# Turning the state update of a gated linear attention kernel: values stationary, keys moving

## The chip, the cores and the metric

The kernel runs on one core of one Trainium2 chip. The time is that of the device for one execution, in microseconds; where several runs were made, their median. Matrix products run on TensorE (PE), elementwise work on VectorE (DVE) and ScalarE (ACT), gathers and scatters are issued by GpSimd (POOL), and SyncE (SP) issues the other DMAs.

## The reference

A layer norm without weights gives `xn` for 4 sequences of 2048 tokens of width 256. The result is `x + attention(xn) + experts(xn)`. The attention is gated and linear, with 8 heads, keys of 128 and values of 64:

```python
state = at[..., None, None] * state + kt[..., None] * vt[:, :, None, :]   # per head: 128 x 64
out_t = jnp.einsum('bhk,bhkv->bhv', qt, state)
...
return out * jax.nn.sigmoid(x @ Wog) @ Wo
```

The experts are 64, of which each token takes 8 by a grouped top-k; each expert takes at most 256 tokens, in the order of their positions, through `silu(g) * u` and a down product, weighted and summed.

## The kernel before, in words

The sequences are cut in 16 chunks of 128 tokens; a step works on one chunk of all four sequences (b = 0 to 3). In a step, the scan over time becomes matrix products: the scores of a chunk are weighted by decays (`Dt`) and multiplied by the values, the state from earlier chunks is read through scaled queries (`outputs`, L773 to L791), and the state is brought forward (`update`, L794): for each head and sequence the transposed keys, weighted by the decay to the chunk's end (`kw`), times the values. `kw` comes from `keys_back` (L755), which transposes the keys on PE into bank 3, and `keys_weighted`, which is on ACT (L980) in the steps of kind norm, count and slots and on DVE (L1379) in the expert steps. `update` writes bank 6, two heads side by side, and DVE's `pair_state` (L1412) decays the state of a pair of heads and adds the bank.

Beside the attention each step carries other work; its kind says which. Steps 0 to 4 ("norm") normalise and route three chunks each. Step 5 ("count") counts the experts' tokens, step 6 ("slots") builds the lists of slots: POOL compares (`reach_group`), PE multiplies pairs of experts (`slot_pair`, L693) and DVE counts them (`count_pair`, L1337). Steps 7 to 14 ("experts") run eight experts each, one a slot; step 15 is "last".

Within a step (`step` of PE, L889) there are eight slots, s = 1 to 8, one for a head. A slot transposes keys and makes scores for head s - 1, transposes the tokens of an expert (L842), projects the next head's queries and keys (L719), runs the expert's gate and up product (L852), in even slots the outputs of a pair, and then the update of head s - 1. Slot 8 has no query and key projection. Every engine runs its own instructions in the written order; semaphores join them (`kw_cp`: weighted keys are there; `u_ps`: the update's products; `state_up`; `oi_ps`: outputs; `v_cp`; `wo_cp`). Places 0 to 4 in `beside` are the points between which the other work of a slot is put.

In an expert slot ACT copies the projections and the transposed tokens, then takes the sigmoid of the expert's gate (`expert_gate`, L1072), then rounds the next expert's weights (`weights_high_e`, L1063). DVE makes the hidden values (L1454, L1456), the weights' remainder (`weights_low_e`, L1460), the gated outputs (L1410), the state (L1423, L1426), and the tokens' remainder (`tokens_low_e`, L1465), for which the next expert product waits. SP issues loads in one order (L416): `load_carry` after the outputs of a pair, `load_decay`, and `next_expert` (L411) after an expert's down product.

Of the kernel before, what the change touches and what calls it, by code (L numbers as in the profile page):

```python
# [13 lines left out]
ALU = mybir.AluOpType  # L14
# [55 lines left out]
def at(c, per, k):  # L70

    return c * per + k


def build(nc, x_in, Wq, Wk, Wv, Wo, Wg, bg, Wog, gate_w, gate_bias, w_gate, w_up, w_down, out):
    with ExitStack() as ctx:
# [42 lines left out]
        kw = sb("kw", [P, B, DK])  # L119
# [158 lines left out]
        state_scaled, state_up = sem("state_scaled"), sem("state_up")  # L278
        gate_done, g_high, g_low = sem("gate_done"), sem("g_high"), sem("g_low")
# [28 lines left out]
        def tokens_bank(c, k):  # L308
            return bank[6] if is_first(c) and k == 1 else bank[7]

# [321 lines left out]
        def _(pe):  # L632
# [122 lines left out]
            def keys_back(c, h):  # L755
                pe.wait_ge(qk_cp, at(c, 16, 2 * h + 2))
                if not (isinstance(c, int) and c == 0 and h == 0):
                    pe.wait_ge(kw_cp, at(c, 8, h))
                for b in range(B):
                    last = tr(bank[3][:, b * P:(b + 1) * P], kT[:, h % 2, b * P:(b + 1) * P], ident[:, :])  # L760
                last.then_inc(kt_ps, 1)
# [32 lines left out]
            def update(c, h):  # L794
                pe.wait_ge(kw_cp, at(c, 8, h + 1))
                if h > 0 and h % 2 == 0:
                    pe.wait_ge(state_up, at(c, 4, h // 2))
                if h == 0 and not (isinstance(c, int) and c == 0):
                    pe.wait_ge(wo_cp, 4 * c)
                for b in range(B):  # L800
                    lo = (h % 2) * B * DV + b * DV
                    last = mm(bank[6][:, lo:lo + DV], kw[:, b, :], V[:, b, h * DV:(h + 1) * DV],  # L802
                              start=True, stop=True)
                if h % 2:
                    last.then_inc(u_ps, 1)

            def out_proj(c, b):

                to = out_bank(c, b)
                if b == 0:  # L810
                    pe.wait_ge(g_low, 4 * c)
                if isinstance(c, int) and c == C - 1:
                    pe.wait_ge((kw_cp, state_up)[b // 2], (8, 4)[b // 2] * (C - 1))
                elif b == 1:
                    pe.wait_ge(state_up, 4 * c)
                elif b > 1:
                    pe.wait_ge(wo_cp, 4 * (c - 1) + b - 1)
                for j in range(KO):
                    for i, (part, other) in enumerate(PARTS):
                        last = mm(to, gT[:, part, j, b * P:(b + 1) * P], wo[:, other, j, :],  # L820
                                  start=(j + i == 0), stop=(j == KO - 1 and i == 2))
                last.then_inc(wo_ps, 1)
# [66 lines left out]
            def step(c, kind):  # L889
# [19 lines left out]
                if not is_last(c):  # L909
                    keys_back(c, 0)  # L910
# [6 lines left out]
                for s in range(1, H + 1):  # L917
                    if s > 1 and not is_last(c):
                        keys_back(c, s - 1)
# [9 lines left out]
                    if s in og_slots(kind):  # L929
                        proj_og(c, kind, og_slots(kind).index(s))  # L930
# [5 lines left out]
                    if s < H:  # L936
                        proj_qk(c, kind, s, 1)
                    beside(c, kind, s, 2)
                    if s % 2 == 0:
                        outputs(c, s // 2 - 1)  # L940
                    beside(c, kind, s, 4)
                    if not is_last(c):
                        update(c, s - 1)
# [21 lines left out]
        def _(act):  # L965
# [14 lines left out]
            def keys_weighted(c, h):  # L980
                act.wait_ge(scan_done, at(c, 8, h + 1))
                act.wait_ge(kt_ps, at(c, 8, h + 1))
                for b in range(B):
                    ins = f(kw[:, b, :], bank[3][:, b * P:(b + 1) * P], ACT.Copy, scale=Dt[:, h, b, P - 1:P])
                ins.then_inc(kw_cp, 1)
# [65 lines left out]

            def outs_high(c, p):
                act.wait_ge(gate_done, at(c, 4, p) + 1)
                f(gT[:, 0, p, :], gated[:, :], ACT.Copy).then_inc(g_high, 1)
# [19 lines left out]
            def beside(c, kind, s, place):  # L1074
# [21 lines left out]
                if kind == "experts" and s > 0 and place == 2:  # L1096
                    expert_gate(c, s - 1)
                    if s < H:
                        weights_high_e(c, s)

            def step(c, kind):
# [24 lines left out]
                for s in range(1, H + 1):  # L1126
# [10 lines left out]
                    if s < H:  # L1137
                        qk_copy(c, kind, s, 1)
                    if kind == "norm" and s % 3 == 0:
                        normalise(STEP_N * c + 1 + s // 3)  # L1140
                    if s in og_slots(kind) and kind == "count":
                        og_gate(c, kind, og_slots(kind).index(s))
                    beside(c, kind, s, 2)
                    if s % 2 == 0:
                        outs_high(c, s // 2 - 1)
# [13 lines left out]
        def _(dve):  # L1159
# [219 lines left out]
            def keys_weighted(c, h):  # L1379
                dve.wait_ge(scan_done, at(c, 8, h + 1))  # L1380
                dve.wait_ge(kt_ps, at(c, 8, h + 1))
                tt(kw[:, :, :], bank[3][:, :].rearrange("p (b d) -> p b d", b=B),
# [29 lines left out]
            def pair_state(c, p):  # L1412

                both = state[:, 2 * p:2 * p + 2].rearrange("p u b v -> p (u b) v")
                added = bank[6][:, :].rearrange("p (r v) -> p r v", v=DV)
# [10 lines left out]
                tt(both, both, added, ALU.add).then_inc(state_up, 1)  # L1426
# [103 lines left out]
            def step(c, kind):  # L1530
# [8 lines left out]
                for s in range(1, H + 1):  # L1539
# [30 lines left out]
                    if s % 2 == 0:  # L1570
                        pair_gated(c, s // 2 - 1)
                        if not is_last(c):
                            pair_state(c, s // 2 - 1)
# [52 lines left out]
```

## Time and profile before

| | us |
|---|---|
| median of 3 runs | 1312.73 (1310.9 to 1312.99) |
| profiled execution | 1313.61 |
| its span | 1311.9 |
| PE busy | 1285.5 |
| DVE busy | 954.0 |
| ACT busy | 556.4 |
| POOL busy | 505.6 |

The page gives each engine's busy time, the chain of work that ended last and the costliest groups; the timeline gives start and length of instructions, merged where they are of one kind. PE's records overlap: a record's length is its latency, and what it costs in a stream is read from start to start. A bracket at the end of a timeline row is the idle time of the engine before it and what ended it. PEld rows are the weight loads.

### The profile page before, as it was taken

To read this page: it belongs to the slowest core of one execution; us is meant where nothing else is said; L and a number is where in the kernel's file an instruction comes from. 1 tells how busy PE (TensorE), PEld (TensorE's weight loads), DVE (VectorE), ACT (ScalarE), POOL (GpSimd) and SP (SyncE) were. 2 spreads that over 40 slices of the span, in tenths; PEclk is the share of its full clock that TensorE was granted. 3 is DMA by queue.
4 is the path that set the end of the run, shared out by engine and by line. 5 is a ranking of instruction groups with operands and counts; after the bars stand their busy time and mean duration, and the time that the engine had idled before them with its cause. 6 is when DMAs were issued, how large, how long until landed. Compare 5 with 4: busy or idle time off the path is not lost.

```text
span 1311.9 us, 27512 instructions
## 1 busy us (share of the span) xinstructions
PE 1285.5 (98%) x9478; PEld 1131.3 (86%) x9478; DVE 954.0 (73%) x2431; ACT 556.4 (42%) x1139; POOL 505.6 (39%) x405
## 2 busy tenths in 40 slices
PE   7999999999999999999999999999999999999999
PEld 6788888888888887799898898998988989989987
DVE  6987978888896659957667577676785776767844
ACT  6566556555653433333333333333333333333322
POOL 2110100110010039637356366274573653745710
PEclk8999999999999999999999999999999999999999
DMA  7565535363442212157576486575774756656755
GB/s 239 178 241 189 176 113 174 101 193 118 153 166 70 81 49 81 34 166 165 126 168 172 99 196 138 129 170 128 171 171 107 194 130 159 165 125 160 173 175 194
DMA packets 124919, 194.66 MB, mean 148 GB/s; under 512 B 12016, under 2 KB 98608, under 8 KB 124592
## 3 DMA queue, kind: packets, MB, share of 16 engines
q1 hardware_dynamic: 94384, 147.99, 34.7%
q0 software_dynamic: 30464, 45.83, 19.1%
q8 instruction: 32, 0.52, 0.2%
q14 instruction: 39, 0.32, 0.1%
HBM read 148.62 MB, written 57.74 MB: 157 GB/s over the span
## 4 chain that ended last, share of the span: by engine, by line
PE 80%; DVE 12%; issue 3%; DMA 2%; POOL 1%; ACT 1%; SPq 0%; DVEq 0%; ACTq 0%; POOLq 0%
PE bank L719 21%; PE bank L802 7%; PE bank L769 7%; PE bank L852 7%; PE bank L734 6%; PE bank L820 6%; PE bank L751 5%; PE bank L787 5%; PE bank L861 4%; PE bank L790 4%; PE bank L760 3%; PE bank L842 2%; DVE Dt L1367 2%; DVE At L1388 2%; POOL sel_all L599 1%
## 5 line engine op out<-in xcount | busy, mean ns | idle before, releaser
L575 POOL DMA_INDIRECT acc<-arena,idx_all x128 | 216.5, 1692 | 129.2 <-issue 68.0
L567 POOL DMA_INDIRECT arena<-table,idx_all x132 | 161.0, 1220 | 201.6 <-ACT share L1060 146.6
L719 PE MATMUL bank<-xp,wq 128*128 128x512 f32 x768 | 215.0, 415 | 0.0
L719 PE MATMUL bank<-xp,wk 128*128 128x512 f32 x768 | 203.9, 400 | 0.2 <-DVE wk L1288 0.2
L719 PEld LDWEIGHTS bank<-xp,wk 128*128 128x128 f32 x768 | 141.1, 188 | 34.1 <-DVE wk L1288 0.6
L719 PEld LDWEIGHTS bank<-xp,wq 128*128 128x128 f32 x768 | 141.0, 190 | 28.6 <-issue 0.5
L1367 DVE TENSOR_TENSOR_SCAN Dt<-decay,eye_b 128x512 f32<-128x512 f32 x128 | 158.1, 1236 | 0.6 <-DMA decay<-decay_dram 0.6
L769 PE MATMUL bank<-qT,kT 128*128 128x128 f32 x1024 | 136.2, 276 | 2.5 <-DVE At L1388 2.5
L1040 ACT ACTIVATE qT<-bank 128x512 f32<-128x512 f32 x128 | 76.6, 598 | 133.8 <-PE bank L719 133.8
L769 PEld LDWEIGHTS bank<-qT,kT 128*128 128x128 f32 x1024 | 125.8, 193 | 3.4 <-DVE At L1388 2.8
L802 PEld LDWEIGHTS bank<-V,kw 128*128 128x128 f32 x960 | 117.5, 191 | 11.7 <-issue 9.8
L802 PE MATMUL bank<-V,kw 128*128 128x64 f32 x960 | 126.8, 275 | 0.0
L1040 ACT ACTIVATE kT<-bank 128x512 f32<-128x512 f32 x128 | 76.5, 597 | 114.8 <-PE bank L719 114.5
L1388 DVE TENSOR_TENSOR At<-bank,Dt 128x512 f32<-128x512 f32 x128 | 87.7, 685 | 34.7 <-PE bank L769 32.9
L544 POOL DMA_DIRECT2D table<-arena x16 | 12.4, 776 | 250.1 <-DVE arena L1272 250.1
L787 PE MATMUL bank<-At,V 128*64 128x128 f32 x1024 | 101.2, 279 | 7.6 <-DVE At L1388 7.6
L1454 DVE TENSOR_TENSOR arena<-bank,arena 128x256 f32<-128x256 f32 x64 | 27.2, 425 | 108.3 <-ACT arena L1072 108.3
L852 PEld LDWEIGHTS bank<-xgT,wgu_p 128*128 128x128 f32 x768 | 97.8, 188 | 9.0 <-issue 3.6
L734 PE MATMUL bank<-wv,xp 128*128 128x512 f32 x384 | 104.6, 408 | 0.2 <-DVE xp L1282 0.2
L751 PE MATMUL bank<-xp,wog 128*128 128x512 f32 x384 | 101.7, 400 | 0.0
L852 PE MATMUL bank<-xgT,wgu_p 128*128 128x256 f32 x768 | 99.5, 279 | 2.0 <-DVE xgT L1465 1.9
L820 PEld LDWEIGHTS bank<-wo,gT 128*128 128x128 f32 x720 | 93.2, 188 | 5.5
(160 smaller groups left out, 2262.1 us busy)
## 6 DMA issues: line engine op xcount, KB each, us to landing
decay<-decay_dram SPq DMA_DIRECT2D x64, 512.0 KB, 5.6
carry<-decay_dram SPq DMA_DIRECT2D x60, 512.0 KB, 4.6
arena<-in_L_attn_x_dram SPq DMA_DIRECT2D x16, 512.0 KB, 4.4
table<-arena SPq DMA_DIRECT2D x16, 512.0 KB, 3.7
xT_dram<-arena SPq DMA_DIRECT2D x16, 512.0 KB, 3.0
arena<-in_L_ffn_w_gate_dram SPq DMA_DIRECT2D x64, 128.0 KB
arena<-in_L_ffn_w_up_dram SPq DMA_DIRECT2D x64, 128.0 KB
arena<-in_L_ffn_w_down_dram SPq DMA_DIRECT2D x64, 128.0 KB
```

The lines of the kernel that those rows point to most:

```text
L567: pool.indirect_dma_start(out=xg[:, e % 2, j, :], out_offset=None, in_=table[:, :], in_offset=bass.IndirectOffsetOnAxis(ap=idx_all[:, e, j ...
L575: pool.indirect_dma_start(out=acc[:, :], out_offset=bass.IndirectOffsetOnAxis(ap=idx_all[:, e, j:j + 1], axis=0), in_=yb[:, e % 2, j, :], ...
L719: last = mm(to[:, :], w[:, part, k, h * DK:(h + 1) * DK], xp[:, other, k, :], start=(k + i == 0), stop=(k == KD - 1 and i == 2))
L734: last = mm(to[:, :], xp[:, part, k, b * P:(b + 1) * P], wv[:, other, k, :], start=(k + i == 0), stop=(k == KD - 1 and i == 2))
L751: last = mm(to[:, :], wog[:, part, k, j * P:(j + 1) * P], xp[:, other, k, :], start=(k + i == 0), stop=(k == KD - 1 and i == 2))
L769: last = mm(bank[2][:, b * P:(b + 1) * P], kT[:, h % 2, b * P:(b + 1) * P], qT[:, h % 2, b * P:(b + 1) * P], start=True, stop=True)
L787: last = mm(bank[5][u * DV:(u + 1) * DV, b * P:(b + 1) * P], V[:, b, h * DV:(h + 1) * DV], At[:, u, b, :], start=True, stop=is_first(c))
L802: last = mm(bank[6][:, lo:lo + DV], kw[:, b, :], V[:, b, h * DV:(h + 1) * DV], start=True, stop=True)
L820: last = mm(to, gT[:, part, j, b * P:(b + 1) * P], wo[:, other, j, :], start=(j + i == 0), stop=(j == KO - 1 and i == 2))
L852: last = mm(expert_bank[j % 2][:, m * CAP:(m + 1) * CAP], wgu_p[:, part, m, k * I:(k + 1) * I], xgT[:, other, k * CAP:(k + 1) * CAP], star ...
L1040: f(dst[:, h % 2, :], bank_of(kind, "qk"[which], h)[:, :], ACT.Copy, scale=scale).then_inc(qk_cp, 1)
L1367: dve.tensor_tensor_scan(Dt[:, h, :, :].rearrange("p b t -> p (b t)"), decay[:, (h // 2) % 2, (h % 2) * BP:(h % 2 + 1) * BP], eye_b[:, :, ...
```

## The change

From the count step to the last expert step (kinds count, slots, experts) the update of a pair of heads is formed the other way round. The values are the stationary operand, 64 columns on one half of the array for each head of the pair; the weighted keys move, 128 columns; the products of both heads and four sequences fill bank 3 (`update_turned`), ahead of the outputs of the pair. ACT copies the bank to SBUF (`update_copy`), into the second of now two buffers of `kw`. After the outputs PE transposes the copy back, four blocks of 128 x 128, into bank 6 (`update_back`), and DVE adds it in the order in which the blocks lie. `keys_back` waits for the copy before it writes bank 3 again. In the expert steps `weights_high_e` comes after `update_copy` on ACT; in count PE's gate projection comes after the second projection of the slot. The first product of the last step waits for `ut_cp`.

```diff
-        kw = sb("kw", [P, B, DK])
+        kw = sb("kw", [P, 2, B, DK])
+        added_t = kw[:, 1, :, :]
...
+        def turned(kind):
+            return kind in ("count", "slots", "experts")
...
-            def keys_back(c, h):
+            def keys_back(c, kind, h):
                 pe.wait_ge(qk_cp, at(c, 16, 2 * h + 2))
                 if not (isinstance(c, int) and c == 0 and h == 0):
                     pe.wait_ge(kw_cp, at(c, 8, h))
+                if turned(kind) and h % 2 == 0:
+                    wait_past(pe, ut_cp, 4 * (c - S_COUNT) + h // 2)
...
+            def update_turned(c, p):
+
+                pe.wait_ge(kw_cp, at(c, 8, 2 * p + 2))
+                pe.wait_ge(v_cp, 4 * c + 4)
+                for b in range(B):
+                    for u in range(2):
+                        h = 2 * p + u
+                        last = mm(bank[3][u * DV:(u + 1) * DV, b * P:(b + 1) * P], V[:, b, h * DV:(h + 1) * DV],
+                                  kw[:, u, b, :], start=True, stop=True)
+                last.then_inc(ut_ps, 1)
+
+            def update_back(c, p):
+
+                pe.wait_ge(ut_cp, 4 * (c - S_COUNT) + p + 1)
+                if p > 0:
+                    pe.wait_ge(state_up, at(c, 4, p))
+                else:
+                    pe.wait_ge(wo_cp, 4 * c)
+                for b in range(B):
+                    last = tr(bank[6][:, b * P:(b + 1) * P], added_t[:, b, :], ident[:, :])
+                last.then_inc(u_ps, 1)
...
-                    pe.wait_ge((kw_cp, state_up)[b // 2], (8, 4)[b // 2] * (C - 1))
+                    pe.wait_ge((ut_cp, state_up)[b // 2], 4 * (C - 1 - (0, S_COUNT)[b < 2]))
...
-                    if s in og_slots(kind):
+                    if s in og_slots(kind) and kind != "count":
                         proj_og(c, kind, og_slots(kind).index(s))
...
                     if s < H:
                         proj_qk(c, kind, s, 1)
+                    if s in og_slots(kind) and kind == "count":
+                        proj_og(c, kind, og_slots(kind).index(s))
                     beside(c, kind, s, 2)
+                    if s % 2 == 0 and turned(kind):
+                        update_turned(c, s // 2 - 1)
                     if s % 2 == 0:
                         outputs(c, s // 2 - 1)
                     beside(c, kind, s, 4)
-                    if not is_last(c):
+                    if s % 2 == 0 and turned(kind):
+                        update_back(c, s // 2 - 1)
+                    if kind == "norm":
                         update(c, s - 1)
...
+            def update_copy(c, p):
+                act.wait_ge(ut_ps, 4 * (c - S_COUNT) + p + 1)
+                f(added_t.rearrange("p b d -> p (b d)"), bank[3][:, :], ACT.Copy).then_inc(ut_cp, 1)
...
                 if kind == "experts" and s > 0 and place == 2:
                     expert_gate(c, s - 1)
-                    if s < H:
-                        weights_high_e(c, s)
+                if kind == "experts" and 0 < s < H and place == 3:
+                    weights_high_e(c, s)
...
+                    if s % 2 == 0 and kind in ("count", "slots"):
+                        update_copy(c, s // 2 - 1)
...
                     beside(c, kind, s, 2)
+                    if s % 2 == 0 and kind == "experts":
+                        update_copy(c, s // 2 - 1)
+                    beside(c, kind, s, 3)
                     if s % 2 == 0:
                         outs_high(c, s // 2 - 1)
...
+                summed, added = both, bank[6][:, :].rearrange("p (r v) -> p r v", v=DV)
+                if turned(kind):
+                    summed = state[:, 2 * p:2 * p + 2]
+                    added = bank[6][:, :].rearrange("p (b u v) -> p u b v", b=B, u=2)
...
-                tt(both, both, added, ALU.add).then_inc(state_up, 1)
+                tt(summed, summed, added, ALU.add).then_inc(state_up, 1)
```

## Rows read from the trace of the kernel before

**Rows 1.** The page: busy time by engine, and the chain that ended last.
```profile
PE 1285.5 (98%) x9478; PEld 1131.3 (86%) x9478; DVE 954.0 (73%) x2431; ACT 556.4 (42%) x1139; POOL 505.6 (39%) x405
...
PE 80%; DVE 12%; issue 3%; DMA 2%; POOL 1%; ACT 1%; SPq 0%; DVEq 0%; ACTq 0%; POOLq 0%
```

**Rows 2.** Windows: length, busy PE, PEld, DVE, ACT, POOL, clock, DMA share, GB/s.
```profile
468.00:552.00 84.00, 80.28 (x598) 63.50 (x596) 68.37 (x335) 26.30 (x60) 64.76 (x64) 0.98 0.15 55
552.00:1247.00 695.00, 693.00 (x5124) 623.59 (x5122) 480.71 (x813) 246.75 (x488) 384.38 (x265) 1.00 0.63 152
```

**Rows 3.** Groups: line, engine, out<-in, shapes, count, busy us, mean ns, idle.
```profile
L1040 ACT ACTIVATE qT<-bank 128x512 f32<-128x512 f32 x128 | 76.6, 598 | 133.8 <-PE bank L719 133.8
...
L802 PEld LDWEIGHTS bank<-V,kw 128*128 128x128 f32 x960 | 117.5, 191 | 11.7 <-issue 9.8
...
L787 PEld LDWEIGHTS bank<-At,V 128*64 128x64 f32 x1024 | 61.4, 136 | 19.8 <-issue 6.0 <-DVE carry L1400 5.2 <-DVE At L1388 3.9
```

**Rows 4.** Timeline of an odd expert slot: start, length, engine, line, operation.
```profile
836.20 1.00 PE L802 MATMUL bank<-V,kw 128*128 128x64 f32 x8
837.03 0.61 PE L760 MATMUL bank<-ident,kT 128*128 128x128 f32 x4
837.48 1.06 PE L769 MATMUL bank<-qT,kT 128*128 128x128 f32 x8
```

**Rows 5.** Timeline of an even expert slot, PE with ACT and DVE.
```profile
862.77 0.44 PE L787 MATMUL bank<-At,V 128*64 128x128 f32 x4
...
863.15 0.62 ACT L1067 ACTIVATE wgu_p<-arena 128x512 fp32r<-128x512 f32 x1
...
863.47 0.39 PE L790 MATMUL bank<-carry,state 128*64 128x128 f32 x4
...
864.35 0.39 PE L790 MATMUL bank<-carry,state 128*64 128x128 f32 x4
864.66 1.10 PE L802 MATMUL bank<-V,kw 128*128 128x64 f32 x8
864.78 0.69 DVE L1410 TENSOR_TENSOR gated<-bank,og 128x512 f32<-128x512 f32 x1
...
865.61 0.61 PE L760 MATMUL bank<-ident,kT 128*128 128x128 f32 x4
```

**Rows 6.** Timeline: slots 7 and 8 of an expert step without late weights.
```profile
628.17 1.54 PE L852 MATMUL bank<-xgT,wgu_p 128*128 128x256 f32 x12
...
632.98 0.69 DVE L1465 TENSOR_TENSOR xgT<-bank,xgT 128x512 fp32r<-128x512 f32 x1
...
634.40 1.53 PE L852 MATMUL bank<-xgT,wgu_p 128*128 128x256 f32 x12
```

**Rows 7.** Waits from 559 to 1247 us: in total, times, longest.
```profile
ACT wgu_p L1067 <- DMA arena<-in_L_ffn_w_down_dram: 16.8, 22, 2.2
...
PE bank L852 <- DVE xgT L1465: 1.9, 3, 1.0
```

**Rows 8.** Timeline: slot 8 of an expert step with late weights.
```profile
808.69 0.68 DVE L1465 TENSOR_TENSOR xgT<-bank,xgT 128x512 fp32r<-128x512 f32 x1
...
809.52 1.61 PE L852 MATMUL bank<-xgT,wgu_p 128*128 128x256 f32 x12 [0.69 <-DVE xgT L1465]
```

**Rows 9.** Timeline of SP's queue: slots 6 and 7 of the same step.
```profile
796.31 0.35 SPq L390 DMA_DIRECT2D carry<-decay_dram  x1
...
799.98 0.38 SPq L395 DMA_DIRECT2D arena<-in_L_ffn_w_gate_dram  x1
```

**Rows 10.** The slots step: a window of DVE, and rows of the timeline.
```profile
510.00:530.00 20.00, 19.86 (x105) 1.00 0.14 54
...
535.21 0.69 DVE L1410 TENSOR_TENSOR gated<-bank,og 128x512 f32<-128x512 f32 x1 [0.57 <-PE bank L790]
...
545.16 1.11 PE L760 MATMUL bank<-ident,kT 128*128 128x128 f32 x4
...
546.07 1.91 PE L769 MATMUL bank<-qT,kT 128*128 128x128 f32 x8
```

More of the change, by code:

```diff
@@ L278, in build @@
         state_scaled, state_up = sem("state_scaled"), sem("state_up")
+        ut_ps, ut_cp = sem("ut_ps"), sem("ut_cp")
         gate_done, g_high, g_low = sem("gate_done"), sem("g_high"), sem("g_low")
@@ L801, in update @@
                     lo = (h % 2) * B * DV + b * DV
-                    last = mm(bank[6][:, lo:lo + DV], kw[:, b, :], V[:, b, h * DV:(h + 1) * DV],
+                    last = mm(bank[6][:, lo:lo + DV], kw[:, h % 2, b, :], V[:, b, h * DV:(h + 1) * DV],
                               start=True, stop=True)
@@ L909, in step @@
                 if not is_last(c):
-                    keys_back(c, 0)
+                    keys_back(c, kind, 0)
                 scores(c, 0)
@@ L918, in step @@
                     if s > 1 and not is_last(c):
-                        keys_back(c, s - 1)
+                        keys_back(c, kind, s - 1)
                     if s > 1 and not is_last(c):
@@ L983, in keys_weighted @@
                 for b in range(B):
-                    ins = f(kw[:, b, :], bank[3][:, b * P:(b + 1) * P], ACT.Copy, scale=Dt[:, h, b, P - 1:P])
+                    ins = f(kw[:, h % 2, b, :], bank[3][:, b * P:(b + 1) * P], ACT.Copy, scale=Dt[:, h, b, P - 1:P])
                 ins.then_inc(kw_cp, 1)
@@ L1381, in keys_weighted @@
                 dve.wait_ge(kt_ps, at(c, 8, h + 1))
-                tt(kw[:, :, :], bank[3][:, :].rearrange("p (b d) -> p b d", b=B),
+                tt(kw[:, h % 2, :, :], bank[3][:, :].rearrange("p (b d) -> p b d", b=B),
                    Dt[:, h, :, P - 1:P].broadcast_to([P, B, DK]), ALU.mult).then_inc(kw_cp, 1)
@@ L1410, in pair_gated, with pair_state @@
                 tt(gated[:, :], bank[5][:, :], og[:, p, :], ALU.mult).then_inc(gate_done, 1)
-            def pair_state(c, p):
+            def pair_state(c, kind, p):
                 both = state[:, 2 * p:2 * p + 2].rearrange("p u b v -> p (u b) v")
-                added = bank[6][:, :].rearrange("p (r v) -> p r v", v=DV)
+                summed, added = both, bank[6][:, :].rearrange("p (r v) -> p r v", v=DV)
+                if turned(kind):
+                    summed = state[:, 2 * p:2 * p + 2]
+                    added = bank[6][:, :].rearrange("p (b u v) -> p u b v", b=B, u=2)
                 if is_first(c):
@@ L1572, in step @@
                         if not is_last(c):
-                            pair_state(c, s // 2 - 1)
+                            pair_state(c, kind, s // 2 - 1)
                     beside(c, kind, s, 4)
```

## The prediction

> **What bounds the kernel now.** I read the page's share of busy time and its chain of waits first: the tensor engine (PE) is busy 98% of the span and carries 80% of the chain that ended last, the vector engine (DVE) 12% [rows 1]. An average over stages could hide a stretch in which PE is not the limit, so the windows come next. From 552 to 1247 us, the eight steps that also run the experts, PE is busy for 693.0 of 695 us while DVE has 481 and ScalarE (ACT) 247: an engine microsecond saved on PE is a microsecond of time there, unless a wait comes up behind it. From 468 to 552 us, mostly the step that builds the slot lists, PE has 80.3 of 84 us, but DVE counts without a break, 19.86 of 20 us in its middle [rows 2, 10]: PE's work is hidden there. Then the timeline of PE, for what one head's update costs and what follows it, and last the waits of two places, since that is where a faster PE would collide.
>
> **What is removed.** In a turned step the four products of a head are issued with the keys stationary, 128 columns, and 64 columns of values moving. The trace has two matmul records for each (fp32), 8 a head. Their weight loads take 191 ns in a record, those of half the columns 136 to 137 [rows 3]. By starts, the odd slot's update occupies PE from 836.20 to 837.03, 0.83 us, the even slot's from 864.66 to 865.61, 0.95 us [rows 4, 5]. A pair costs 1.78 us.
>
> **What is added on PE.** The turned product has V as stationary operand on 64 columns, alternating between the halves, and 128 moving columns: that is exactly the first half of the outputs (L787). There a group of four records (two halves, two records each) starts 0.22 us after the one before: from 863.47 to 864.35 lie four such steps, 0.88 us [rows 5]. A turned pair has 16 records, so four groups, 0.88 us. The change from whole to half array and back (0.31 us from the start of the last half group to the update, where 0.22 would be its own) is paid once at each end of the outputs today, and once at each end of turned product plus outputs afterwards, so it adds nothing. The four transposes back are the kind of L760: 0.45 us from 837.03 to 837.48 [rows 4]. Together 1.33 us, a saving of **0.45 us a pair**. The steps from count to the last expert step are ten, so 40 pairs and 18.0 us at most: 14.4 in the expert steps, 1.8 in count, 1.8 in slots.
>
> The row says that a transpose costs PE 0.11 us in a stream, although each record lasts longer because they overlap. A rule of the Trainium skill speaks against this (TensorE: Matmul & The Clock Gate, Part 4, PE-mode transpose): about 275 ns for a transpose in a kernel's context, and the fast clock does not engage for it. By that, four would take 1.10 us, a pair would lose 0.20 and 40 pairs 8 us, for 1321. The starts of rows 4 contradict it for this stream, with whole expert windows at a granted clock of 1.00, and I go by them.
>
> **The copy and the order.** On ACT one copy of a bank to SBUF is added per pair, of the shape that takes 598 ns [rows 3]. In an even expert slot PE would begin the turned product at 862.77 and end it 0.88 later, at 863.65; a consumer starts some 0.2 us after its producer (gated at 864.78, while the last group that it needs starts at 864.35 and lasts 0.22), so the copy runs from 863.86 to 864.46. PE meanwhile does the outputs, and reaches the transposes at 863.65 + (864.66 - 862.77) = 865.54 [rows 5]. Cover 0.9 us: the new wait costs nothing; if the copy were that much later, PE would stand still and everything behind it too. The expert's sigmoid stands before it on ACT, waits only for the expert product that ends at 862.77, and is over when the weights' copy starts at 863.15. Behind it is now the rounding copy of the next weights (863.15 before, 864.46 after, 1.3 later), and DVE's subtraction behind that, so gated and the state follow 1.2 us later. PE's own even slot is 0.38 us longer (0.88 + 0.45 - 0.95), so DVE falls back by 0.8 against PE, into idle time (481 of 695 busy); nothing is charged, and up to 0.8 us a pair is its price without that cover. The add on DVE reads the same 512 elements in another order; I take no change, between nothing and a tenth more of one instruction off the path. The second buffer of keys, the swapped gate projection in the one count step and the exchanged semaphore at the last step change no amount of work: nothing.
>
> **What eats the gain in the experts.** The slot saved 0.83 us is the odd one, the loss of 0.38 lies in the even one. After slot 7 comes slot 8, which has no query and key projection, and DVE's chain to the split tokens is nearly its bound. In a good step the two expert products start at 628.17 and 634.40, 6.23 us apart; the split tokens that the second needs are ready at 632.98 + 0.69 = 633.67, and a start follows a release by 0.15 (808.69 + 0.68 to 809.52) [rows 6, 8]. So DVE allows 5.65 and PE would want 6.23 - 0.83 = 5.40: 0.25 lost. In four of the eight steps the weights come late by DMA, and the product starts just as it is released (three of them with an idle time, 1.9 us in all [rows 7], as at 809.52 [rows 8]); there the whole 0.83 is lost. 4 x 0.25 + 4 x 0.83 = 4.3 us. Then the queue of SP: it issues the carry and decay loads when the outputs of slot 6 end (796.31), the weights after slot 7's expert down product (799.98) [rows 9]. The first moves 0.88 later and the second only 0.38, so half a megabyte twice stands 0.5 us closer ahead of the weights. ACT waited for weights 22 times already [rows 7]. Bounds for this: 0, and 8 x 0.5 = 4.0; I take 2.5, since it is the place where waits are already frequent. Expert steps: 14.4 - 4.3 - 2.5 = **7.6 us**.
>
> **Count and slots.** In count PE is the limit and no slack is short: **1.8 us**. In slots DVE is the limit, so what PE saves is not seen, and the turned product now stands 0.88 us ahead of outputs for which DVE already waits (0.57 us at 535.21). Ends: a gain of 1.8, and a loss of 4 x 0.88 = 3.5 plus one more stretch at the slow clock; there is one now, after a wait, in which four transposes need 0.91 us from 545.16 (to 546.07) and their row 1.11 instead of 0.61 [rows 10]; the window's mean clock of 0.98 over 84 us says that it cost 0.02 x 84 = 1.7 us. From -1.8 to +5.2; I take a **loss of 1.3 us**, nearer to the middle, because only the even slots whose start is tied to DVE or GpSimd pass it on.
>
> **Sum.** 7.6 + 1.8 - 1.3 = 8.1 us. The profiled execution took 1313.61 us (span 1311.9); less 8.1 is 1305.5. The median of the runs is 0.88 lower (1312.73), so 1304.6 us.
>
> **The rivals.**
> A, the transposes run slowly: with the 0.91 us of rows 10 a pair costs 0.88 + 0.91 = 1.79, nothing is gained anywhere, and slots lose 1.3: 1314. For it: they are the most of what is new on PE. Against: all transposes of the expert steps [rows 4, 5]. 0.03.
> B, the gain is eaten by waits: slot 8 takes 1.33 in all eight steps (10.6), the other places as in the worst slots case (5.2): 18.0 - 1.8 - 10.6 - 5.2 = 0.4 us gained, 1312.3. For it: rows 7 to 9. Against: DVE idles for 31% of the expert steps. 0.07.
> C, slower: weights arrive late not by 0.5 but by 2 us more in each expert step, because the loads ahead of them and the indirect transfers share the same queues' bandwidth. PE then waits at slot 8 for 0.83 + 2.0 in each of eight steps, 22.6 us, against 14.4 + 1.8 - 1.3 of the rest: 7.7 slower, 1320.4. It decides from 14.9 / 8 = 1.86 us a step. For it: 16.8 us of waits for these weights already. Against: the loads' own time is short against a slot of 10 us, and the fall back on the queue is only 0.5. 0.05.
> D, slower: the alternating halves do not overlap when the keys move. At the 0.104 us a record of the full array (0.83 / 8) a pair costs 1.66 + 0.45 = 2.11, 0.33 more than now, 13 us over 40 pairs: 1326. Against: L787 has the same operands' shapes at 0.055 a record. 0.04.
>
> **From cases to numbers.** The forecast has 0.81. Its own range: best 18.0 - 1.0 (every step a good one, slots gaining), about 1296; worst 1312. 8 in 10 needs less: I give 1298.5 to 1310. What a measurement can tell from no change is about 0.2%, 2.6 us. Faster than 1310.1: nearly all of the forecast, 0.82; same, from A, B and the forecast's worst end, 0.09; slower, C and D, 0.09.
>
> **What would show it.** In the changed trace the turned matmuls (128*64, 128 moving) should have groups of four 0.22 apart; the transposes of the added tile start to start 0.11; no idle time of PE before them, and the copy over before the outputs are. The first matmul of the expert product in slot 8 should have an idle time in all eight steps, 0.3 to 1.5 us, released by the split tokens. The slots stretch should be as long as now or longer, with PE waiting more. I am wrong if PE waits for the copy, if the turned groups run at 0.4, or if PE's idle time in the expert steps stays under 3 us (then the time is nearer to 1299) or passes 15.

## The result: slower by 0.44%, where a gain was forecast

| | before | after |
|---|---|---|
| median, us (runs) | 1313.03 (11) | 1319.47 (11) |
| lowest to highest | 1310.90 to 1315.15 | 1315.33 to 1323.51 |
| profiled execution (span) | 1313.61 (1311.9) | 1316.75 (1315.1) |

The ratio is 1.0044, 95% interval 1.0031 to 1.0057. The forecast was 1304.6 with a range to 1310.0: wrong, in its sign too. The profiled execution of after is 2.7 us under its median, so its trace shows 3.2 us of the 6.4. All times are those of runs at the high granted clock; one run of slots_after (1402.9 us) and one of the kernel before beside it (2110.22 us, mean granted clock 0.556) are left out.

The page after, as in [rows 1]: busy time by engine, and the chain that ended last, by engine.

```profile
PE 1269.2 (97%) x9638; PEld 1109.3 (84%) x9638; DVE 953.4 (73%) x2431; ACT 579.2 (44%) x1179; POOL 503.7 (38%) x405
...
PE 74%; DVE 12%; DMA 5%; issue 4%; POOL 2%; ACT 1%; SPq 1%; DVEq 0%; ACTq 0%
```

PE is busy for 16 us less and gives up six points of the chain; DMA goes from 2 to 5%, and the next line of the page of the profile names it: the expert weights, `arena<-in_L_ffn_w_down_dram`. The windows of after, columns as in [rows 2]:

```profile
468.00:552.00 84.00, 75.36 (x570) 58.62 (x570) 67.09 (x333) 26.43 (x61) 64.24 (x64) 0.98 0.16 52
552.00:1247.00 695.00, 683.34 (x5243) 608.21 (x5244) 479.29 (x811) 265.46 (x521) 379.20 (x263) 1.00 0.63 151
```

In the expert steps PE now stands still for 11.7 of 695 us, where it was 2.0. The waits of after from 559 to 1250 us, as in [rows 7] (total, times, longest):

```profile
ACT wgu_p L1106 <- DMA arena<-in_L_ffn_w_down_dram: 29.0, 21, 2.6
...
PE bank L881 <- DVE xgT L1512: 9.8, 11, 1.7
```

ACT waited 16.8 us for the weights before and waits 29.0 now; PE waited 1.9 us for the split tokens and waits 9.8, of which six times and 7.9 us in slot 8.

The even slot of after, PE and ACT, against [rows 4, 5]. L821 is `update_turned`, L833 `update_back`, L1089 `update_copy`, L797 the second half of the outputs, L767 `keys_back`, L881 the gate and up product, L1106 `weights_high_e`:

```profile
620.25 1.09 PE L821 MATMUL bank<-kw,V 128*64 128x128 f32 x16
621.17 0.39 PE L794 MATMUL bank<-At,V 128*64 128x128 f32 x4
...
622.70 0.39 PE L797 MATMUL bank<-carry,state 128*64 128x128 f32 x4
623.02 0.66 PE L833 MATMUL bank<-ident,kw 128*128 128x128 f32 x4
623.51 0.60 PE L767 MATMUL bank<-ident,kT 128*128 128x128 f32 x4
...
621.39 0.60 ACT L1089 ACTIVATE kw<-bank 128x512 f32<-128x512 f32 x1 [0.65 <-PE bank L821]
```

The turned product takes 0.92 us (forecast 0.88), the four transposes 0.49 (0.45), and the copy is over at 621.99, 1.0 us before PE comes to the transposes (0.9). What was costed on PE and ACT came within 0.04 us a piece.

Where the time of an expert step went is seen by adding PE's groups of instructions from start to start, so that a wait counts to the group ahead of it. Means of seven expert steps, from slot 1 of the first to slot 1 of the last, us a step:

| group | before | after |
|---|---|---|
| update; turned product + transposes back | 7.08 | 3.70 + 1.89 |
| outputs and `keys_back` | 11.13 | 10.91 |
| slot 8: gate projection up to the expert product | 1.95 | 2.68 |
| slot 8: token transposes up to the down product | 0.44 | 0.74 |
| query and key projections, with waits behind them | 23.57 | 23.94 |
| expert products and down products, with waits behind them | 16.95 | 17.16 |
| whole step | 86.94 | 86.88 |

The first two rows save 1.71 us a step, 13.7 in eight; the other four lose 1.61; the groups not listed differ by 0.04. By another mark, the split of a step's tokens on DVE (x_split) to the next one, the eight expert steps last 694.2 us before and 695.0 after (the last of them, outside the means above, 86.5 and 88.1), the count step 76.3 and 74.9, the slots step 87.2 and 89.3. With 1.2 us by which the untouched norm steps and 0.5 by which the last step came out longer in this one trace, that is the 3.2 us: 0.8 - 1.4 + 2.1 + 1.2 + 0.5. (The slots step's 87.2 is high for the old update: before_again, sp_before and carry_late have 86.5, so the change costs 2.8 us there.)

### The profile page after: what moved, and what is told of

The parts are those of the page before. It is cut to its first block, busy times and chain, and to the rows that moved or that the text cites. A ratio compares the mean times of both kernels' runs of the same rounds, so it can differ in the third digit from the quotient of the medians.

```text
span 1315.1 us, 27947 instructions
## 1 busy us (share of the span) xinstructions
PE 1269.2 (97%) x9638; PEld 1109.3 (84%) x9638; DVE 953.4 (73%) x2431; ACT 579.2 (44%) x1179; POOL 503.7 (38%) x405
## 4 chain that ended last, share of the span: by engine, by line
PE 74%; DVE 12%; DMA 5%; issue 4%; POOL 2%; ACT 1%; SPq 1%; DVEq 0%; ACTq 0%
PE bank L724 19%; PE bank L849 6%; PE bank L739 6%; PE bank L776 6%; PE bank L881 6%; DMA arena<-in_L_ffn_w_down_dram 5%; PE bank L756 5%; PE bank L794 4%; PE bank L797 4%; PE bank L890 4%; PE bank L821 3%; PE bank L767 3%; PE bank L871 2%; DVE At L1432 2%; POOL sel_all L604 2%
## 5 line engine op out<-in xcount | busy, mean ns | idle before, releaser
L580 POOL DMA_INDIRECT acc<-arena,idx_all x128 | 220.5, 1723 | 148.8 <-issue 57.8
L572 POOL DMA_INDIRECT arena<-table,idx_all x132 | 155.6, 1179 | 186.1 <-ACT share L1099 128.8
L881 PEld LDWEIGHTS bank<-xgT,wgu_p 128*128 128x128 f32 x768 | 97.0, 188 | 20.6 <-issue 16.3
L881 PE MATMUL bank<-xgT,wgu_p 128*128 128x256 f32 x768 | 100.7, 280 | 9.8 <-DVE xgT L1512 9.8
L549 POOL DMA_DIRECT2D table<-arena x16 | 12.4, 777 | 249.4 <-DVE arena L1316 249.4
L849 PE MATMUL bank<-wo,gT 128*128 128x256 f32 x720 | 94.6, 280 | 0.0
L797 PE MATMUL bank<-carry,state 128*64 128x128 f32 x960 | 93.9, 273 | 0.0
L604 POOL TENSOR_SCALAR sel_all<-arena 64x256 bf16<-64x256 bf16 x64 | 64.2, 1018 | 65.4 <-DVEq L1379 55.3
```

The source lines that it names most:

```text
L572: pool.indirect_dma_start(out=xg[:, e % 2, j, :], out_offset=None, in_=table[:, :], in_offset=bass.IndirectOffsetOnAxis(ap=idx_all[:, e, j ...
L580: pool.indirect_dma_start(out=acc[:, :], out_offset=bass.IndirectOffsetOnAxis(ap=idx_all[:, e, j:j + 1], axis=0), in_=yb[:, e % 2, j, :], ...
L797: last = mm(bank[5][u * DV:(u + 1) * DV, b * P:(b + 1) * P], state[:, 2 * p + u, b, :], carry[:, p % 2, u, b, :], start=False, stop=True)
L881: last = mm(expert_bank[j % 2][:, m * CAP:(m + 1) * CAP], wgu_p[:, part, m, k * I:(k + 1) * I], xgT[:, other, k * CAP:(k + 1) * CAP], star ...
```

## Why the weights are late: one step with a wait, one without

SyncE's queue in after, slots 6 and 7 of two expert steps, with the rounding that needs the weights. Columns: start, length, engine, line, operation. L395 is the carry load, L389 the decay load, L400 the first load of an expert's weights:

```profile
624.58 0.35 SPq L395 DMA_DIRECT2D carry<-decay_dram  x1
625.18 0.33 SPq L389 DMA_DIRECT2D decay<-decay_dram  x1
626.48 0.38 SPq L400 DMA_DIRECT2D arena<-in_L_ffn_w_gate_dram  x1
...
633.74 0.63 ACT L1106 ACTIVATE wgu_p<-arena 128x512 fp32r<-128x512 f32 x1 [2.56 <-DMA arena<-in_L_ffn_w_down_dram]
...
636.21 0.68 DVE L1512 TENSOR_TENSOR xgT<-bank,xgT 128x512 fp32r<-128x512 f32 x1
...
637.04 1.61 PE L881 MATMUL bank<-xgT,wgu_p 128*128 128x256 f32 x12 [1.67 <-DVE xgT L1512]
...
796.60 0.34 SPq L395 DMA_DIRECT2D carry<-decay_dram  x1
797.20 0.33 SPq L389 DMA_DIRECT2D decay<-decay_dram  x1
799.82 0.38 SPq L400 DMA_DIRECT2D arena<-in_L_ffn_w_gate_dram  x1
...
805.39 0.63 ACT L1106 ACTIVATE wgu_p<-arena 128x512 fp32r<-128x512 f32 x1 [1.15 <-DMA arena<-in_L_ffn_w_down_dram]
```

In the second step the weights are issued 3.22 us behind the carry load (before: 3.67 [rows 9]) and rounded 5.6 us after issue. In the first they stand 1.90 behind it and are rounded 7.3 after issue; from there DVE's remainder, its split of the tokens and the product follow, and PE stands for 1.67 us. The eight steps of after fall in two classes for the load of slot 7: distances (from the issue of the carry load to that of the weights) of 3.0 to 3.4 with 5.0 to 5.7 us to the rounding, and 1.5 to 2.0 with 7.0 to 7.6, four of each. Before, all eight distances are 3.7, with 4.4 to 6.6.

The forecast had the step from 3.67 to 3.2, and there the first class lies. It did not have the second: there the carry load is issued 1.88 us after the start of the last output products (622.70 to 624.58), in the other step 0.57 (796.03 to 796.60), as before (795.74 to 796.31). The carry load waits for nothing but these products. Such late signals are found without the change too (last section); the change took 0.5 us of the distance that had to cover them.

## The experiments

Three theories stood at the start. **Q**, the queue: outputs that end 0.9 us later let SyncE issue carry and decay, a megabyte, right ahead of an odd slot's weights. **V**: the rounding of the weights, moved behind the copy on ACT, pushes DVE back. **S**: the change itself makes the semaphores of PE's products arrive late. The ratios are to the kernel before as it ran beside them (medians 1313.33 for the first four, 1314.30 for the next four, 1314.70 for the last two). Each trace is one execution, up to 6 us off its kernel's median (sp_after 1313.27), so where a trace and a median disagree by a few microseconds the median decides.

| run | median, us | ratio | 95% interval |
|---|---|---|---|
| sp_after | 1306.98 | 0.9953 | 0.9936 to 0.9970 |
| sp_before | 1312.45 | 0.9997 | 0.9986 to 1.0008 |
| weights_first | 1314.75 | 1.0016 | 1.0001 to 1.0032 |
| turned_early | 1317.84 | 1.0033 | 1.0018 to 1.0047 |
| carry_late | 1320.94 | 1.0055 | 1.0038 to 1.0072 |
| sp_wfirst | 1308.58 | 0.9963 | 0.9949 to 0.9976 |
| sp_noslots | 1306.49 | 0.9943 | 0.9924 to 0.9962 |
| before_again | 1312.02 | one run | |
| early_noslots | 1318.93 | 1.0032 | 1.0021 to 1.0044 |
| slots_after | 1307.47 | 0.9959 | 0.9944 to 0.9974 |

### The loads in another order, in both kernels

In the expert steps SyncE issues the weights of slots 3, 5 and 7 one place earlier, ahead of carry and decay. The same edit in after (sp_after) and in before (sp_before), here its second half:

```diff
...
                 if kind == "experts":
-                    next_expert(c, 3)
                     next_expert(c, 4)
+                    next_expert(c, 5)
                 load_carry(c + 1, 0)
...
-                    for j in range(5, ends):
+                    for j in range(6, ends):
```

> The changed kernel with one edit: in the expert steps SyncE issues the weights for slots 3, 5 and 7 before, not after, the carry and decay loads of half a megabyte each. In the changed kernel ACT waits 29.0 us for weights (21 times), before it 16.8, and the products of slot 8 start just as the split tokens release them. Theory Q (the queue: the outputs, and with them the carry load, come later and stand right ahead of the weights): ACT's waits for weights fall under 5 us, the idle time of PE before the expert products falls from 9.8 to under 4, the expert steps shorten by 8 to 12 us, so about 1308. Rival V (the vector engine's chain, put back by the later rounding of the weights, is what starves slot 8): the waits for DMA go, the time does not, 1315 to 1320. Rival S (semaphores of PE arrive late in slots 4 and 6, 1 to 2.3 us after the matmul): gated still starts up to 2.7 us after the last output group; the time moves by less than 4 us.

> The kernel before with the same edit of SyncE's order as sp_after: weights for slots 3, 5 and 7 ahead of the carry and decay loads. It has 16.8 us of ACT waits for weights, but only 1.9 us of them reach PE before the expert products. All theories: 1 to 2 us faster than before at most, or the same. If it is as much faster as sp_after is than the changed kernel, the queue's order is no part of what the change cost.

Measured: after gains 12.5 us by it (1319.47 to 1306.98) and is now faster than before; before gains 0.9, inside its interval. The waits of sp_after, in which the rounding is at L1108 and the product at L883:

```profile
ACT wgu_p L1108 <- DMA arena<-in_L_ffn_w_down_dram: 5.9, 5, 2.5
...
PE bank L883 <- DVE xgT L1514: 3.5, 4, 1.7
```

29.0 us of waits for weights became 5.9, 9.8 of PE's became 3.5, and the expert steps 689.7 us long, 5.3 less where Q expected 8 to 12; this trace is 6.3 us over its median. Q holds: the same edit is worth 12.5 us with the turned update and nothing measurable without it, and with it the turned update is a gain.

### The delay alone, put into the kernel before

carry_late keeps the old update and lets SyncE's carry load of an expert step wait for the update's products instead of the outputs':

```diff
-                sp.wait_ge(oi_ps, 4 * c + p - 1)
+                sp.wait_ge(u_ps if late else oi_ps, 4 * c + p - 1)
```

> The kernel before with one wait exchanged in the expert steps: SyncE's carry load waits for the update that follows a pair's outputs, not for the outputs, so the carry and decay loads are issued 1.3 us later and stand that much closer ahead of the weights; no engine does other work. Theory Q: ACT's waits for weights rise from 16.8 to 25 to 32 us, slot 7 to slot 8 of the expert products goes from 6.57 us on average to 7.2 or more, and the time rises by 4 to 9 us, to about 1319. If the late outputs cost nothing by way of the queue (rivals V and S), the time stays within 2 us of 1313.

Measured: 1320.94, 6.6 us slower. Its queue and its waits:

```profile
798.28 0.34 SPq L390 DMA_DIRECT2D carry<-decay_dram  x1
798.88 0.33 SPq L384 DMA_DIRECT2D decay<-decay_dram  x1
800.92 0.38 SPq L395 DMA_DIRECT2D arena<-in_L_ffn_w_gate_dram  x1
```

```profile
ACT wgu_p L1067 <- DMA arena<-in_L_ffn_w_down_dram: 41.3, 29, 3.9
...
PE bank L852 <- DVE xgT L1465: 8.0, 9, 2.8
```

The distance is 2.6 us instead of 3.7 (1.0 less, not the 1.3 expected; 2.6 in most steps, down to 1.9 in slot 7 and 1.1 in slot 5), and that alone makes the picture of after: ACT's waits 41.3, more than the 25 to 32 expected, PE's 8.0. The expert steps last 702.6. No instruction of PE, ACT or DVE was touched, and no wait for the carry or decay loads themselves appears on them, so the place of these loads ahead of the weights is enough as a cause.

### The rounding ahead of the copy again

```diff
                     expert_gate(c, s - 1)
-                if kind == "experts" and 0 < s < H and place == 3:
-                    weights_high_e(c, s)
+                    if s < H:
+                        weights_high_e(c, s)
```

> The changed kernel with one part undone: ACT rounds the next expert's weights right after the expert's sigmoid again, ahead of the copy of the turned update. Theory Q: the weights that are late are those of odd slots, in which there is no copy, so nothing is gained: within 2 us of the changed kernel. Rival V: the vector engine gets the even slots' weights 1.3 us earlier, its fall back of 0.8 us a pair is gone, and the expert steps shorten by 4 to 8 us. If the copy becomes late instead, PE waits before the transposes and it gets slower.

> The changed kernel with both edits: weights for the odd slots ahead of the carry and decay loads on SyncE, and ACT rounding the weights ahead of the copy of the turned update. The first alone gave 1307.0, the second alone 1314.8, the changed kernel 1319.5. If the queue (Q) and the vector engine's chain (V) are two separate causes, their gains add, and with slot 8 bound by the chain at 5.65 us in place of 6.4 it comes to 1302 to 1305. If V acted only through late weights it stays at 1307.

On after it brings 4.7 us (1314.75), on sp_after nothing (1308.58 against 1306.98, the wrong way). The 4.7 us lie in V's range (4 to 8); Q had expected at most 2 and missed. So the place of the rounding matters while the weights are late, and by the times not otherwise: V is a part of the price of late weights, as sp_wfirst's expectation had it for this outcome. In the profile of weights_first the waits for weights stay at 30.5 us and PE's at 9.3.

### The turned product ahead of the expert product

```diff
+                    if s % 2 == 0 and kind == "experts":
+                        update_turned(c, s // 2 - 1)
                     beside(c, kind, s, 2)
-                    if s % 2 == 0 and turned(kind):
+                    if s % 2 == 0 and turned(kind) and kind != "experts":
                         update_turned(c, s // 2 - 1)
```

> The changed kernel with the turned product of the expert steps moved from just behind the expert product to just ahead of it (after the second projection), its copy on ACT right after the projection's. The same work, but the dense stream of half-array matmuls is cut in two, and the outputs follow the expert product directly as they did before. Theory Q: the outputs end no earlier against the weights of the next slot, so ACT's waits for weights stay at 25 to 30 us, but slot 8's product is called 0.9 us later and so idles less: 3 to 6 us faster. Theory S with density as its cause: the last output group to gated falls back to 0.44 us in slots 4 and 6, the carry load follows at 0.57, and the waits for weights fall to some 17: 8 to 12 us faster, about 1308. If neither matters it stays at 1319.

> sp_noslots (weights ahead of the carry loads, slots step as before) with the turned product of the expert steps moved ahead of the expert product, and its copy right behind the projection's. Theory: with the weights on time, slot 8 is bound by VectorE's chain to the split tokens (5.65 us from slot 7's product by the trace of before; 6.04 measured in sp_noslots), and now PE fills 0.9 us of that wait with the turned product. The expert steps (685.2 us in sp_noslots) shorten by up to 8 x 0.4 to 8 x 0.9, so 1300 to 1304. Rival: the outputs' end and the copy's order matter more, no gain: 1306. Against it speaks that the same move alone gave only 1317.8 from 1319.5.

Both missed. turned_early takes PE's waits for tokens from 9.8 to 0.6 us, keeps ACT's for weights at 25.5, and is at 1317.84, 1.6 us faster than after where Q expected 3 to 6; early_noslots, the same on top of the best version, is 12.4 us slower than it. PE's starts in early_noslots (L826 turned product, L886 expert product, L799 outputs), and below them in sp_noslots, in the old order:

```profile
615.21 1.09 PE L826 MATMUL bank<-kw,V 128*64 128x128 f32 x16
616.23 1.65 PE L886 MATMUL bank<-xgT,wgu_p 128*128 128x256 f32 x12
617.81 0.44 PE L799 MATMUL bank<-At,V 128*64 128x128 f32 x4
```

```profile
806.26 1.65 PE L886 MATMUL bank<-xgT,wgu_p 128*128 128x256 f32 x12
807.84 1.09 PE L826 MATMUL bank<-kw,V 128*64 128x128 f32 x16
808.77 0.39 PE L799 MATMUL bank<-At,V 128*64 128x128 f32 x4
```

Ahead of the outputs, which use half the columns as it does itself, the turned product costs 0.93 us; ahead of the full-width expert product 1.02. Each pair now has two more changes between half and whole array; by the starts the projection ahead of them costs 0.09 us more, the turned product 0.10, the expert product 0.08, the outputs 0.05: 0.32 us a pair, 10 us in 32 pairs. The prediction had counted these changes and found that the order chosen adds none; this pair shows what they would have cost. The Trainium skill (TensorEngine Tiling (Array Packing), Key Properties) says that a change of tiling mode drains the array; these rows fit, at 0.05 to 0.1 us for a group beside such a change, but do not show the drain itself. The expert steps of early_noslots are 20.0 us longer than those of sp_noslots (705.2 and 685.2). The other 10 us are longer gaps behind the projections of slot 7 (0.35 a step), behind the token transposes of slot 8 (0.2) and at the step's end (0.55 a step, the transposes back up to the value projection); why these came was not followed further, and the one trace is 3.5 us over its median.

### The slots step as before, and the turned product elsewhere in it

sp_noslots is sp_after with the slots step's updates as they were; slots_after is sp_after with the turned product behind the outputs in that step:

```diff
-            return kind in ("count", "slots", "experts")
+            return kind in ("count", "experts")
```
```diff
-                    if s % 2 == 0 and turned(kind):
+                    if s % 2 == 0 and turned(kind) and kind != "slots":
                         update_turned(c, s // 2 - 1)
                     if s % 2 == 0:
                         outputs(c, s // 2 - 1)
+                    if s % 2 == 0 and kind == "slots":
+                        update_turned(c, s // 2 - 1)
```

> sp_after with the slots step left as it was before (turned update in count and in the expert steps only). In the changed kernel the slots step took 89.4 us instead of 87.2. Theory: VectorE is the limit there and the outputs come 0.9 us later for it, so this gives back some 2 us: 1305, with the slots step at 87.2. Rival: the clock's fall and the waits are chance, and it stays at 1307.

> sp_after (1307.0) with one edit: in the slots step the turned product is issued behind the outputs of the pair, not ahead of them. Theory: the slots step lengthened from 86.5 to 89.3 us because the outputs, for which VectorE waits there, came 0.9 us later in each of four pairs; so it falls back to 86.5 to 87.5 us, and the time by about 2 us, to 1305. Rival: the step is longer because of the copy and the transposes behind it (ScalarE's order, or PE waiting for the copy without cover): it stays at 89 us or gets longer, 1307 to 1309.

sp_noslots is the fastest version, 1306.49, and beats both kernels: the slots step takes 86.5 us, the expert steps 685.2. sp_after and slots_after, with 89.3 and 88.9 us in that step, overlap with it in their medians (1306.98, 1307.47), so the 2.8 us are shown in the traces and not by the times.

DVE's waits in the slots step, first in after (464.25 to 553.58 us), then in slots_after (462.34 to 551.26):

```profile
DVE gated L1454 <- PE bank L797: 3.2, 3, 1.4
```

```profile
DVE state L1477 <- PE bank L835: 2.5, 3, 1.0
DVE gated L1458 <- PE bank L799: 1.1, 2, 0.6
```

With the old update DVE waits there 1.1 us for the outputs (in both traces of before, in sp_before and in sp_noslots). In after it is 3.2, and the 2.1 more are the larger part of the 2.8 us between 86.5 and 89.3. Behind the outputs the turned product gives these back, and DVE then waits 2.5 us for the transposes back in its state addition. DVE bounds the step, and PE's longer even slot reaches it by whichever result comes last; the gain expected from the new order (86.5 to 87.5 us) did not come, but went to that second wait, as the rival named.

### The kernel before once more

> The kernel before, unchanged, for its trace. In the traces of the changed kernel and of three experiments, among them sp_before, which has no turned update, semaphore updates of PE come up to 2.3 us after the end of their matmul in slots 4 and 6. If the change makes them late, they are on time here (gated 0.43 us after the start of the last output group); if they belong to the chip or to a run, they are late here too in some slots. Time 1313.

before_again has distances from carry to weights of 1.1 to 4.3 us in slot 5 and 2.6 to 3.7 in slot 7, where the kernel before had 3.7 throughout in its first trace. Its waits:

```profile
ACT wgu_p L1067 <- DMA arena<-in_L_ffn_w_down_dram: 26.6, 25, 2.2
...
PE bank L852 <- DVE xgT L1465: 2.2, 3, 1.1
```

The lag from the last output product to `gated`, which shows the late signals, reaches 3.07 us in slot 4 there, and 2.38 us in slot 6 of sp_before (mean 1.20; after: 1.51, up to 2.12), both with the old update. So the change is not needed for late signals, and S as it was put falls. Whether the change makes them more frequent is open: the semaphore of slot 6's outputs is updated more than 1 us after the start of the last products in 0, 1, 3 and 3 of eight expert steps in the four traces with the old update, and in 1 to 7 in the eight with the turned one, 4 of them in after.

The same trace shows which late weights cost something. The columns are ACT's waits for weights, the part of them in slot 7, PE's waits for the split tokens, the mean from the start of slot 7's expert product to that of slot 8, and the eight expert steps together, all in us:

| trace | ACT | in slot 7 | PE | slot 7 to 8 | eight steps |
|---|---|---|---|---|---|
| before, first trace | 16.8 | 7.4 | 1.9 | 6.57 | 694.2 |
| before_again | 26.6 | 9.0 | 2.2 | 6.57 | 694.1 |
| sp_before | 0.8 | 0.7 | none | 6.27 | 692.4 |
| carry_late | 41.3 | 16.4 | 8.0 | 7.32 | 702.6 |
| after | 29.0 | 13.1 | 9.8 | 7.01 | 695.0 |
| sp_after | 5.9 | 5.9 | 3.5 | 6.41 | 689.7 |
| sp_noslots | 6.5 | 3.5 | 2.1 | 6.04 | 685.2 |

before_again waits for weights nearly as long as after does, and loses nothing by it against the first trace: 7.6 of its 9.8 us more are for the weights of slot 5, which do not reach PE there. What costs time are the waits of slot 7, ahead of slot 8, and they cost more with the turned update: PE arrives at slot 8 earlier by what it saves, all eight products of after start 0.15 us after the split tokens, while four of eight had 0.7 us to spare in the first trace of before.

## Point by point

- **Saving on PE.** 0.45 us a pair forecast, 1.71 / 4 = 0.43 measured; 13.7 of 14.4 us in the expert steps. The transposes cost 0.11 to 0.12 each in the stream, as [rows 4] said, though each record lasts 0.27; rival A falls, and so does the 1321 at 0.275 us each. Rival D falls with the groups at 0.23.
- **The copy.** Cover (the time between the copy's end and PE's need of it) of 0.9 us forecast, 1.0 there; PE waited for it 0.5 us in all. Right.
- **DVE's bound in slot 8.** An idle time in all eight steps was forecast; six have one, and all eight start within 0.2 us of the tokens' end. Its size (4.3 us, of which 8 x 0.25 = 2.0 would stay with the weights in time) came from good steps, and is too small: from sp_before to sp_noslots, both with the weights early, slot 7 to slot 8 shortens by 0.23 of the 0.83 us, so 0.6 is lost in each of eight steps, 4.8 us. The forecast had the tokens ready 5.50 us after slot 7's product begins; in sp_noslots they are at 6.1 to 6.3 in five steps and at 5.3 to 5.6 in three. In four of the five the signal of slot 6's outputs came 1.6 us or more after the last products began, in the fifth the weights were 1.2 us late; in the three it came within 1.0. In sp_before the tokens are at 6.1 in exactly the three steps with signals 2.0 to 2.4 us late, at 5.5 in the others, and there it costs 0.1 us a step. So a late signal also reaches slot 8 without the queue, by DVE, and with the turned update it costs more.
- **The queue term: the step that failed.** I put 2.5 us on "half a megabyte twice stands 0.5 us closer ahead of the weights", bounds 0 and 4.0. The bound took a distance closer by 0.5 to cost at most 0.5. That shift of 0.5 came as forecast, and alone in four of eight steps. In the other four the distance shrank by 1.7 to 2.1, since the carry load itself comes up to 2.2 us after the products, and the rounding started 7.2 us after the issue in their mean, against 5.4 in the mean of before. In the trace of after, slot 8's product starts 7.01 us after slot 7's, not 6.57 - 0.83 = 5.74: 1.27 in each of eight steps, 10.2 us, where the two terms together had 6.8. Taking the term away by the order of the loads returns 12.5 us of median. The mechanism is that of rival C, at a chance of 0.05: late weights at slot 8. That its 1320.4 lies near the 1319.47 is partly luck, for it had 2 us more in each of eight steps and 22.6 us of waits, and its reason, a bandwidth shared with the indirect transfers, was not tested. Its reason against, a fall back of only 0.5 us, took the gap of one step for that of all, and a margin of 3.7 us as harmless where the variation uses it up.
- **"Nothing is charged"** for DVE's fall back of 0.8 us a pair. No cost is seen with the weights issued early (sp_wfirst gains nothing over sp_after), but it is worth 4.7 us with the weights late. It was costed as if the two delays were apart, and they add up in one chain.
- **With the weights in time** the turned update is worth 7.2 us in the expert steps (sp_before's 692.4 to sp_noslots' 685.2). That this is near the forecast's 7.6 is luck: without its queue term the forecast is 14.4 - 4.3 = 10.1, or 12.4 if no step has late weights. DVE's bound above takes 2.8 of the 5.2 us to that; the rest was not followed.
- **Count** 1.8 forecast, 1.4 measured. **Slots** a loss of 1.3 forecast (from -1.8 to +5.2), 2.8 measured against the usual 86.5, by the place named: the outputs behind the turned product, for which DVE waits. The stretch at the lower clock was priced at 1.7 us; the first trace of before, with it (granted clock 0.98), has 87.2 us there, before_again without it (1.00) has 86.5, so it cost at most 0.7.

What the forecast lacked was the question what happens if the distance in [rows 9] halves. The trace of before had it equal in all eight steps, so its spread could not be read there; a second trace of the same kernel, before_again, shows it.

## What to carry to other kernels

An engine's saving moves the places where its signals are sent, and each DMA issued on such a signal moves against those behind it in its queue: list these distances before and after, and price the ones that shrink by the whole chain behind the load, not by the shift. If a load for the critical path stands behind loads that are needed later, put it ahead of them first, and then change the compute. Here the reordering alone brought nothing measurable, the turned update alone lost 6.4 us, and both together with the slots step left alone gained 7.8 (1314.30 to 1306.49).

## What the hardware showed that was not expected

The signal of PE's last output product sometimes comes late at its consumers. The readings of the distances gave SyncE's side: 1.88 us from these products to the carry load in one step, 0.57 in another. DVE's `gated`, which needs the same products, in the same two steps of after:

```profile
624.44 0.69 DVE L1454 TENSOR_TENSOR gated<-bank,og 128x512 f32<-128x512 f32 x1 [1.21 <-PE bank L797]
...
796.03 0.39 PE L797 MATMUL bank<-carry,state 128*64 128x128 f32 x4
...
796.96 0.68 DVE L1454 TENSOR_TENSOR gated<-bank,og 128x512 f32<-128x512 f32 x1
```

In the first step it starts 1.74 us after 622.70, having waited for it; in the second 0.93 after 796.03, straight from other work. Two engines see the same delay. Mean lags of `gated` over the expert steps, from that start, in us (the largest in brackets); a part of them is DVE's own other work:

| | slot 4 | slot 6 |
|---|---|---|
| before, first trace | 0.45 (0.54) | 0.55 (0.80) |
| before_again | 1.72 (3.07) | 0.77 (1.53) |
| sp_before | 0.56 (0.93) | 1.20 (2.38) |
| after | 1.50 (2.67) | 1.51 (2.12) |
| sp_after | 0.53 (0.82) | 1.46 (2.12) |

The late signal moves with the order of the loads (in slot 4 the lag is at most 0.94 us in the six traces with the weights first, and 2.4 to 3.1 at its largest in five of the other six), which hints at something that the queues share, but no run here tells what it is. It differs between traces of one kernel, and so may be what spreads the times of after over 8 us, where before has 4; that was not tested.
